# Attention over 128 graphs: its chunks start at slot 0 of the next step instead of slot 3

## What is computed

```
h = max(layernorm(x), 0)
q, k, v = h Wq + bq, h Wk + bk, h Wv + bv        (split into 12 heads)
scores = q k^T / sqrt(32) + beta * adj           (-9e15 where adj <= 0)
out = x + softmax(scores) v
```

## Time and profile before

| | before |
|---|---|
| median of three executions | 1017.1 us |
| profiled execution | 1016.69 us |
| its span (first to last instruction) | 1014.8 us |
| PE busy | 972.9 us (96%) |
| DVE busy | 902.9 us (89%) |
| ACT busy | 908.4 us (90%) |
| POOL busy | 809.5 us (80%) |
| mean granted TensorE clock | 0.991 |
| HBM read, written | 35.91 MB, 25.17 MB |

### The profile page before, as it was taken

The page is one execution under the profiler, slowest core; times in us unless marked ns, Lnnn a source line. Parts: engine busy times, 40 slices in busy tenths (PEclk is TensorE's granted clock), DMA queues, the critical chain, the costliest instruction groups (busy, mean ns, idle before and its releaser), DMA issues. The chain is left out here.

```text
span 1014.8 us, 33454 instructions
## 1 busy us (share of the span) xinstructions
PE 972.9 (96%) x10587; PEld 671.9 (66%) x10587; DVE 902.9 (89%) x4193; ACT 908.4 (90%) x2392; POOL 809.5 (80%) x1003
## 2 busy tenths in 40 slices
PE   3789999999999999999999999999999999999996
PEld 1346677766677766667766667776667776666764
DVE  5659999999999999999999999999999999998897
ACT  5369999999999999999999999999999999999897
POOL 3778888888888888888888888888888888888661
PEclk9989999999999999999999999999999999999998
DMA  7787799988879998778987777998788999877731
GB/s 227 107 153 158 164 171 167 184 154 164 168 169 182 161 165 180 162 163 175 171 178 158 165 170 159 183 160 180 160 167 168 176 166 174 161 125 149 147 99 40
DMA packets 234352, 163.15 MB, mean 161 GB/s; under 512 B 109760, under 2 KB 234176, under 8 KB 234176
## 3 DMA queue, kind: packets, MB, share of 16 engines
q1 hardware_dynamic: 233904, 160.62, 80.9%
q10 hardware_dynamic: 272, 0.39, 0.1%
HBM read 35.91 MB, written 25.17 MB: 60 GB/s over the span
## 5 line engine op out<-in xcount | busy, mean ns | idle before, releaser
L599 ACT ACTIVATE probs<-biased,neg_max 128x128 f32<-128x128 f32 x1536 | 491.9, 398 | 65.6 <-DVE neg_max L726 58.2
L516 PE MATMUL ps_p<-hT,w 128*128 128x512 f16 x1728 | 417.8, 382 | 10.5 <-DMA hT<-h_parts 8.9
L726 DVE CUSTOM_DVE_ANT_0 biased<-ps_s,mask 128x128 f32<-128x128 f32 x1536 | 355.5, 287 | 65.3 <-PE ps_s L528 40.3
L516 PEld LDWEIGHTS ps_p<-hT,w 128*128 128x128 f16 x1728 | 169.3, 98 | 163.5 <-issue 13.1
L732 DVE TENSOR_TENSOR pT<-ps_t,pT 128x512 f16<-128x512 f32 x384 | 263.3, 686 | 0.4 <-ACT pT L633 0.3
L536 PE MATMUL ps_t<-ident,probs 128*128 128x128 f32 x1536 | 246.1, 283 | 3.9
L633 ACT ACTIVATE pT<-ps_t 128x512 f16<-128x512 f32 x384 | 224.1, 584 | 0.4 <-PE ps_t L536 0.4
L516 PE MATMUL ps_p<-w,hT 128*128 128x384 f16 x1152 | 207.7, 327 | 1.0 <-DVE w L765 1.0
L528 PEld LDWEIGHTS ps_s<-k_st,q_st 96*128 96x128 f16 x1536 | 117.8, 97 | 80.2 <-DVE neg_max L726 5.9
L536 PEld LDWEIGHTS ps_t<-ident,probs 128*128 128x128 f32 x1536 | 161.2, 141 | 7.8 <-ACT probs L599 7.1
L551 PE MATMUL ps_o<-v,pT 128*128 128x33 f16 x1536 | 157.4, 179 | 4.4 <-DVE pT L732 4.3
(11 more groups left out here) (66 smaller groups left out, 1172.3 us busy)
## 6 DMA issues: line engine op xcount, KB each, us to landing
q_st<-qT SPq DMA_DIRECT2D x288, 128.0 KB, 3.3
k_st<-kT SPq DMA_DIRECT2D x288, 128.0 KB, 4.9
out<-on SPq DMA_DIRECT2D x128, 192.0 KB, 3.2
xs<-in_x SPq DMA_DIRECT2D x31, 768.0 KB, 5.0
adjs<-in_adj SPq DMA_DIRECT2D x32, 256.0 KB, 5.4
hT<-h_parts SPq DMA_TRANSPOSE x62, 4.6
k_st<-in_L_gnn_Wk SPq DMA_DIRECT2D x1, 576.0 KB, 5.8
k_st<-in_L_gnn_Wq SPq DMA_DIRECT2D x1, 576.0 KB, 6.9
```

Source lines behind the costliest of these rows:

```text
L516: mm = pe.matmul(dst, stationary, moving, start=m == 0, stop=m == MMS - 1)
L599: act.activation(probs[:, odd, i, :], biased[:, odd, i, :], ACT.Exp, bias=neg_max[:, odd, i:i + 1], scale=-1.0).then_inc(exp_done, 1)
L726: dve.tensor_tensor_reduce(out=biased[:, odd, i, :], in0=ps_s[:, i * N:(i + 1) * N], in1=mask[:, gp, v // CH, :], scale=-1.0, scalar=3.0e3 ...
```

## The change

`LAG` becomes 0: the chunks of step s-1 have their scores in slots 0 to 11 of step s, and the loops after the last projection run for 12 + 3 slots. A graph's division comes three slots earlier counted from its projection, so the `store` and `add_x` calls of SP and POOL keep their places in the written order and work on the next graph. In SP's queue k stack 2 follows k stack 1 directly; the load of the adjacency and a store come behind it.

```diff
-    LAG = CH
+    LAG = 0
...
 def step(s, par):        # sync engine
                 if 2 <= s <= STEPS:
-                    store(s - 2, 1)
+                    store(s - 2, 2)
...
-                    store(s - 2, 2)
+                    store(s - 2, 3)
...
-                if 2 <= s <= STEPS:
-                    store(s - 2, 3)
+                if attend:
+                    store(s - 1, 0)
                 if proj:
                     spread(s, par, "k", 0)
                     spread(s, par, "k", 1)
+                    spread(s, par, "k", 2)
                 if 0 <= s <= STEPS - 2:
                     sp.wait_ge(mask_done, s + 1)
                     sp.nop(nofuse=True)
                     sp.dma_start(adjs[:], adj_v[s + 1]).then_inc(adj_in, 16)
                 if attend:
-                    store(s - 1, 0)
-                if proj:
-                    spread(s, par, "k", 2)
+                    store(s - 1, 1)
                 if s == STEPS:
-                    for j in range(1, G):
+                    for j in range(2, G):
                         store(s - 1, j)
...
 def step(s, par):        # gpsimd
                 if older:
-                    add_x(s - 2, par, 2)
+                    add_x(s - 2, par, 3)
...
-                if older:
-                    add_x(s - 2, par, 3)
+                if attend:
+                    add_x(s - 1, 1 - par, 0)
...
                 if attend:
-                    add_x(s - 1, 1 - par, 0)
+                    add_x(s - 1, 1 - par, 1)
...
                 if attend:
-                    add_x(s - 1, 1 - par, 1)
+                    add_x(s - 1, 1 - par, 2)
                 if s == STEPS:
-                    add_x(s - 1, 1 - par, 2)
                     add_x(s - 1, 1 - par, 3)
```

## The result

The changed kernel takes 1135.0 us (median of 4 runs, 1131.32 to 1138.91), the kernel before beside it 1017.01 us: a ratio of 1.1165, 95% interval 1.1139 to 1.1192. It is slower by 118 us. The forecast had the direction and named the wait and the clock, but 1092 us and a range of 1060 to 1124 us were too low; rival C (the clock falls at each wait) had 1131 us.

A forecast was written before the change was run, and what follows sets the result against it. The prediction took PE's own work to set the period, so PE's waits add in full. From 1016.7 us it summed - 2.5 (ends) + 66 (waits at slot 0) + 12 (clock) = 1092 us, range 1060 to 1124.

The forecast's parts named there:

- rival C: At slot 0: the clock falls at each wait, 66 + 51 us, giving 1131 us; chance 14%.
- part 2: PE's wait at slot 0 for k's stack 2: 30 waits of 2.2 us, a cost of 66 us.
- part 3: TensorE clock at the slot 0 waits: halves at one wait in three, 10 x 1.2 = 12 us cost.
- Part 1: Ends of the run: three slots fewer after the last projection, -5.3 + 2.8 = -2.5 us.
- two pitches: Stack 2's lateness at slot 0: 2.55 us with stack 1's landing pitch, 1.8 with stack 2's own; 2.2 taken.
- only SP's 1.3 us are earned: Upper bound of the slot 0 wait: the reorder gains only SP's earlier issue, 3.7 - 1.3 = 2.4 us.
- starts over when PE starts over: Chain from slot 0 through q stack 0 and SP's queue to stack 2: unchanged, so each step pays its own wait.
- Rival A: At slot 0: the waits come but the clock stays, 1016.7 - 2.5 + 66 = 1080 us; chance 26%.
- Rival B: At slot 0: stack 2 lands in time, no wait, only the gain at the ends, 1014.2 us; chance 6%.
- Rival D: At slot 0: waits of 0.1 us eat the gain only, 1017 us, no change; chance 4%.
- Part 4: Masks, the load of `adjs`, stores, `add_x` and slot content on ACT and DVE: costed at nothing.

## Why the prediction was wrong

The forecast sum had the right parts, and two of its terms were too small: the waits of part 2, 66 us where counting from slot 0 to slot 0 gives 30 x 3.0 = 90, and the clock of part 3, 12 us where it gives 32.

**Part 1, the ends, held.** -2.5 us was forecast. In the kernel with the waits split, step 2 starts 84.57 - 82.12 = 2.45 us later than before (2.8 forecast), and the time from the top of step 31, the last with a projection, to the end is 63.86 - 58.61 = 5.25 us shorter (5.3 forecast). That is -2.8 us, and the medians, 1013.4 against 1016.2 us, differ by as much.

**Part 2, the wait, held in kind and place: 30 waits, all for k, each ended by the last landing of stack 2.** Its size was 2.2 us and was too small: PE idles 2.57 us a top (77 us for 66), and behind a top at full clock stack 2 lands 2.9 us later than the 29.96 us after which PE could use it. Two things went wrong in that term. I took stack 1's landing as in before, but behind a top at full clock it lands 30.4 us after slot 0 in the changed kernel and 29.9 us in before; why, no run here shows. Stack 2 follows 2.5 us later. And I took a value between two pitches. Worked again from each landing in the trace of before, their sums give 2.3 us with stack 1's pitch and 2.0 us with stack 2's, not 2.55 and 1.8. The larger was the nearer: in the kernel with the waits split, where nothing waits for it, stack 2 is 2.7 us late. What I took as the upper bound, 2.4 us by "only SP's 1.3 us are earned", was no bound, as my own 2.55 already said: the reorder earned 1.0 us of 3.7. That the chain "starts over when PE starts over" was right for the seven steps whose top the clock passes at full speed: q stack 0 is issued 7.65 us after slot 0, as before the change. Where the clock falls, it is issued 9.0 to 10.3 us after it.

**Part 3, the clock, is the step whose reasoning failed, and not only its size.** It took "one wait in three: 10 x 1.2 = 12 us". Measured: 23 stretches and 44.2 us of additional PE time, 1.9 us each, of which some 32 us, 1.4 us each, lengthen the run. The price was near, the number of falls was not. The earlier trace rows held the warning: a fall 2.7 us after PE's last matmul. I put against it that PE is dense on both sides of the wait. The changed kernel shows that this does not help: the clock falls at 23 of 30 tops, at the top of step 16 2.3 us after PE stopped (559.32 - 557.00). The runs with matmuls in the wait show that the idle time does it. And the falls feed the sum: a slow slot 0 delays q and everything behind it, and the next landing of stack 2 comes 34.3 instead of 32.9 us after slot 0. I had the low stretches of before as a term with one wait in three and as rival C at 14%; nothing in the rows spoke for one in three. Neither error alone would have taken the time out of the range: with 90 us for the waits the sum is 1116 us, with 32 us for the falls it is 1112 us; with both it is 1136 us.

**Rival C** came to 1131 us partly by luck: its waits are too short, as mine were, and it lets the clock fall at all 30 tops at 1.7 us, where 23 fell at 1.4. **Rival A** (the clock stays) is met nearest by the run with ten matmuls: 1105 us, not 1080, since the waits are longer.

**Rival B** (no wait) needed a landing within 2.8 us; the fastest DMA to `k_st` in the changed kernel's steps took 2.9 us, half of them 4.8 or more, and in the step shown above the last of stack 2 took 5.5. The Trainium skill, page "DMA: Bandwidth & Descriptors", section on the anatomy of one DMA, gives a fixed 2.0 us plus bytes over 436 GB/s for DMAs issued from GpSimd, by which 128 KB would take an estimated 2.3 us. The DMAs here, issued by SP, took 2.9 us or more. Rival **D** fell with B.

**Part 4** held: masks, loads and stores cost nothing; the run with the new order alone is at 0.9996, and with the waits split a step takes 29.98 us.

## What to carry to other kernels

Before a consumer is moved closer to a transfer, read the landing, not the issue, against the new place of use in every step, and let the consumer wait for the part that it needs first; here a semaphore for each part turned 118 us of loss into 3 us of gain. A reorder in the queue can earn less than the issue times suggest: here an issue 1.3 us earlier brought a landing 1.0 us earlier. A short wait of TensorE that comes every step must be priced twice, once as idle time and once as work at half clock behind it; the two overlap in part, so the price is read from slot 0 to slot 0.

## What the hardware showed that was not expected

Idle times of 1.96 to 4.02 us on PE, once in a step that is otherwise dense, brought the granted clock to 0.50 for 3.4 us, sometimes 6.8, at 23 of 30 places; why waits of 2.27, 2.29 and 3.64 us passed at full clock stays open. Ten matmuls without any use in that place left 2 falls and made the changed kernel 30 us faster. And the DMAs to `k_st`, 128 KB each between two places on the chip, took from 2.9 to 6.9 us from issue to landing in the steps of one kernel. What is queued before them is part of it: one DMA transpose less moved the landing of stack 2 by 2.2 us (32.7 to 30.5), about half of it by an earlier issue.
